# Last stage of a graph network kernel: residual adds on GpSimd, ScalarE on two groups, reciprocals by group

## What is computed

```python
exp_e = jnp.exp(e)                                     # e: score of each edge and head
denom = jax.ops.segment_sum(exp_e, trg, num_segments=n)
alpha = exp_e / (denom[trg] + 1e-10)
msg = h_prime[src] * alpha[:, :, None]
out = jax.ops.segment_sum(msg, trg, num_segments=n)    # (n, 8 * 32)
...
x = x + out                                            # x: (6250, 256) f32, the result
```

## Time and profile before

| | |
|---|---|
| median of 3 runs | 3204.86 us (3203.37 to 3205.41) |
| the profiled execution, span from first to last instruction | 3208.5 us |
| busy, share of the span: PE, DVE, ACT, POOL | 78%, 69%, 46%, 62% |
| from the start of the reciprocal (L1855) to the end of the span | 3174.19 to 3208.5 us |
| mean HBM traffic over the span | 116 GB/s |

### The profile page before, as it was taken

One profiled execution on the slowest core, in us unless ns is written; L12 is line 12 of the kernel. 1 busy time (PEld: TensorE's weight loads), 2 busy tenths in 40 slices (PEclk: granted clock), 3 DMA queues, 4 the chain that ended last, 5 costly groups with the idle time before them and its releaser, 6 DMA issues. The chain is left out here.

```text
span 3208.5 us, 81208 instructions
## 1 busy us (share of the span) xinstructions
PE 2491.2 (78%) x25602; PEld 2177.9 (68%) x25603; DVE 2207.3 (69%) x4515; ACT 1489.5 (46%) x3803; POOL 1998.7 (62%) x2143
## 2 busy tenths in 40 slices
PE   0577777777777699999999999966777777777773
PEld 0466666666666589999999999954555555555552
DVE  7777778877777646666666666647666667776766
ACT  5444444444444368888888888841111111111113
POOL 4677777777777534444444444427777777777772
PEclk9998889999989999999999999977889878889886
DMA  6555555555555400000000000006555655555554
GB/s 155 171 157 157 153 159 167 168 155 158 162 157 157 128 5 20 20 20 20 20 19 19 19 19 19 20 25 184 172 173 172 172 172 172 172 172 172 172 170 132
DMA packets 183839, 373.70 MB, mean 116 GB/s; under 512 B 42597, under 2 KB 93687, under 8 KB 183768
## 3 DMA queue, kind: packets, MB, share of 16 engines
q0 software_dynamic: 75552, 209.66, 23.1%
q1 hardware_dynamic: 107392, 162.37, 17.0%
q10 hardware_dynamic: 824, 0.87, 0.1%
HBM read 346.95 MB, written 25.80 MB: 116 GB/s over the span
## 5 line engine op out<-in xcount | busy, mean ns | idle before, releaser
L449 POOL DMA_INDIRECT rows<-tab_scratch,srcs x784 | 766.8, 978 | 238.7 <-issue 232.0
L1449 POOL DMA_INDIRECT a_rows<-tab_scratch,srcs x784 | 750.6, 957 | 251.9 <-issue 235.2
L1515 PE MATMUL sum_ps<-feat,a_hot 128*125 128x264 f32 x1960 | 608.8, 467 | 234.2 <-DVE feat L1607 116.5
L1515 PEld LDWEIGHTS sum_ps<-feat,a_hot 128*125 128x125 f32 x1960 | 423.3, 226 | 340.7 <-DVE feat L1607 128.6
L875 PE MATMUL z_ps<-ah,w 128*128 128x125 f16 x6400 | 553.6, 219 | 0.0
L875 PE MATMUL z_ps<-al,w 128*128 128x125 f16 x3200 | 542.4, 217 | 0.0
L875 PEld LDWEIGHTS z_ps<-ah,w 128*128 128x128 f16 x6400 | 489.6, 97 | 0.0
L1459 ACT ACTIVATE feat<-d 128x32 f32<-128x32 f32 x196 | 44.9, 229 | 826.5 <-DVE d L1603 578.9
L503 PE MATMUL mlp_ps<-ewa,eab 128*128 128x256 f16 x788 | 199.9, 287 | 266.4 <-PEq L499 265.1
L510 PE MATMUL sum_ps<-rows,hot 128*125 128x256 f16 x980 | 294.0, 300 | 81.5 <-DMA rows<-tab_scratch,srcs 56.1
L1059 ACT ACTIVATE a<-z,pack 128x125 f32<-128x125 f32 x800 | 321.5, 480 | 72.5 <-ACTq L1055 72.5
(11 more groups left out here) (206 smaller groups left out, 5533.7 us busy)
## 6 DMA issues: line engine op xcount, KB each, us to landing
ea<-edge_t SPq DMA_DIRECT2D x394, 128.0 KB
dstb<-dst_flat SPq DMA_DIRECT2D x98, 512.0 KB, 4.0
rows<-tab_scratch,srcs POOLq DMA_INDIRECT x784
a_rows<-tab_scratch,srcs POOLq DMA_INDIRECT x784
tab_scratch<-prow SPq DMA_DIRECT2D x50, 128.9 KB
hx<-x SPq DMA_DIRECT2D x50, 125.0 KB
x_scratch<-x SPq DMA_DIRECT2D x50, 125.0 KB
hs<-tab_scratch SPq DMA_DIRECT2D x50, 125.0 KB
```

What stands on the lines that cost most here:

```text
L449: pool.indirect_dma_start(rows[:, b % DEEP, k, :], None, dram["tab0"], bass.IndirectOffsetOnAxis(ap=srcs[:, c:c + 1], axis=0),).then_inc(r ...
L1449: pool.indirect_dma_start(rows[:, b % DEEP, k, :], None, dram["tab1"], bass.IndirectOffsetOnAxis(ap=srcs[:, c:c + 1], axis=0),).then_inc(r ...
L1515: ins = pe.matmul(out[:], hot[:, h, k, :], feat[:, row, k, :], start=(k == 0), stop=(k == CB - 1))
```

## The change

Five things change, all in `finish`:

- ScalarE multiplies groups 4 and 8 in place of 3, 6 and 9 and waits for each group's weights.
- GpSimd gets a program: it does the residual add and the tail for the groups 1, 4, 6 and 8 (`ON_POOL`), in this order. For 4 and 8 it waits for ScalarE (`normed`), for 1 and 6 for VectorE's multiply (`weighted`). It raises `pool_out`.
- VectorE takes the reciprocals by groups of 40 columns: first 4 and 0, then each group's own just before its multiply, and 8's after group 1's multiply. It multiplies eight groups and adds six. It no longer waits for ScalarE.
- SP stores in the order 0, 2, 1, 3, 4, 5, 7, 6, 9, 8, waiting for `pool_out` or `out_ready`.
- The slice of a group gets a helper, `chunk`.

```diff
--- before.py
+++ after.py
@@ -1787,11 +1787,19 @@
         top_ps = m.ps("top_ps", [P, 1])
 
         out_ready = m.sem("out_ready")
-        ON_ACT = (3, 6, 9)
+        ON_ACT = (4, 8)
+        ON_POOL = (1, 4, 6, 8)
+        FIRST_G = (4, 0)
+        STORES = (0, 2, 1, 3, 4, 5, 7, 6, 9, 8)
+        fits = 2 * D - TW
+
+        def chunk(i):
+            return slice(i * FB, (i + 1) * FB)
         out_stored = m.sem("out_stored")
         mx_ready, turned, mrow_ready, top_done = m.sem("mx_ready"), m.sem("turned"), m.sem("mrow_ready"), m.sem("top_done")
         exp_in, exp_ready = m.sem("exp_in"), m.sem("exp_ready")
         g_ready, normed = m.sem("g_ready"), m.sem("f_normed")
+        weighted, pool_out = m.sem("f_weighted"), m.sem("pool_out")
         chain_sem = m.sem("f_chain")
         HALF = 112
 
@@ -1800,9 +1808,12 @@
         @block.sync
         def _(sp):
             out_v = out.rearrange("(t p) c -> p t c", p=TN)
-            for i in range(steps):
-                tiles = slice(i * FB, (i + 1) * FB)
-                sp.wait_ge(out_ready, i + 1)
+            for i in STORES:
+                tiles = chunk(i)
+                if i in ON_POOL:
+                    sp.wait_ge(pool_out, ON_POOL.index(i) + 1)
+                else:
+                    sp.wait_ge(out_ready, len([j for j in range(i + 1) if j not in ON_POOL]))
                 for rows in (slice(0, HALF), slice(HALF, TN)):
                     sp.dma_start(out_v[rows, tiles, :], acc[rows, tiles, 0:D]).then_inc(out_stored, 16)
             sp.wait_ge(out_stored, 32 * steps)
@@ -1812,13 +1823,24 @@
             act.wait_ge(exp_in, 1)
             act.sem_inc(exp_in, -1)
             act.activation(g[:], c[:], ACT.Exp).then_inc(exp_ready, 1)
-            act.wait_ge(g_ready, 1)
-            for i in ON_ACT:
+            for n, i in enumerate(ON_ACT):
+                act.wait_ge(g_ready, n + 1)
                 for k in range(i * FB, (i + 1) * FB):
                     for h in range(HEADS):
                         a = acc[0:TN, k, h * HD:(h + 1) * HD]
                         ins = act.activation(a, a, ACT.Copy, scale=g[:, k, h:h + 1])
                 ins.then_inc(normed, 1)
+
+        @block.gpsimd
+        def _(pool):
+            for n, i in enumerate(ON_POOL):
+                a = acc[0:TN, chunk(i), 0:D]
+                if i in ON_ACT:
+                    pool.wait_ge(normed, ON_ACT.index(i) + 1)
+                else:
+                    pool.wait_ge(weighted, len([j for j in ON_POOL[:n + 1] if j not in ON_ACT]))
+                pool.tensor_tensor(a[:, :, 0:fits], a[:, :, 0:fits], acc[0:TN, chunk(i), TW:2 * D], ALU.add)
+                pool.tensor_tensor(a[:, :, fits:D], a[:, :, fits:D], x1_tail[:, chunk(i), :], ALU.add).then_inc(pool_out, 1)
 
         @block.tensor
         def _(pe):
@@ -1852,19 +1874,31 @@
             dve.wait_ge(exp_ready, 1)
             dve.sem_inc(exp_ready, -1)
             settled(dve.scalar_tensor_tensor(out=g[:], in0=g[:], scalar=GUARD, in1=acc[0:TN, :, D:TW], op0=ALU.mult, op1=ALU.add))
-            settled(dve.reciprocal(g[:], g[:]))
-            dve.sem_inc(g_ready, 1)
-            fits = 2 * D - TW
+
+            def weights(i):
+                settled(dve.reciprocal(g[:, chunk(i), :], g[:, chunk(i), :]))
+
+            for i in FIRST_G:
+                weights(i)
+                if i in ON_ACT:
+                    dve.sem_inc(g_ready, 1)
             for i in range(steps):
-                tiles = slice(i * FB, (i + 1) * FB)
-                a = acc[0:TN, tiles, 0:D]
+                a = acc[0:TN, chunk(i), 0:D]
                 a4 = a.rearrange("p t (h f) -> p t h f", h=HEADS)
-                if i in ON_ACT:
-                    dve.wait_ge(normed, ON_ACT.index(i) + 1)
-                else:
-                    settled(dve.tensor_tensor(a4, a4, g[:, tiles, :].unsqueeze(3).broadcast_to([TN, FB, HEADS, HD]), ALU.mult))
-                dve.tensor_tensor(a[:, :, 0:fits], a[:, :, 0:fits], acc[0:TN, tiles, TW:2 * D], ALU.add)
-                dve.tensor_tensor(a[:, :, fits:D], a[:, :, fits:D], x1_tail[:, tiles, :], ALU.add).then_inc(out_ready, 1)
+                if i not in ON_ACT:
+                    if i not in FIRST_G:
+                        weights(i)
+                    ins = dve.tensor_tensor(a4, a4, g[:, chunk(i), :].unsqueeze(3).broadcast_to([TN, FB, HEADS, HD]), ALU.mult)
+                    if i in ON_POOL:
+                        ins.then_inc(weighted, 1)
+                    else:
+                        settled(ins)
+                if i not in ON_POOL:
+                    dve.tensor_tensor(a[:, :, 0:fits], a[:, :, 0:fits], acc[0:TN, chunk(i), TW:2 * D], ALU.add)
+                    dve.tensor_tensor(a[:, :, fits:D], a[:, :, fits:D], x1_tail[:, chunk(i), :], ALU.add).then_inc(out_ready, 1)
+                if i == 1:
+                    weights(ON_ACT[1])
+                    dve.sem_inc(g_ready, 1)
 
 
 _PLAIN = ["x", "L0_gnn_eps", "L0_gnn_ee_w1", "L0_gnn_ee_b1", "L0_gnn_ee_w2", "L0_gnn_ee_b2", "L1_gnn_W"]
```

## The result

The changed kernel takes 3230.29 us (3228.89 to 3231.68, five runs), the kernel before beside it 3205.41 us (3203.37 to 3207.66). The ratio is 1.007, with a 95% interval of 1.0059 to 1.0081: slower by 19 to 26 us. The profiled execution has a span of 3227.1 us; its own time was 3228.89 us, 1.8 us above the span.

The account below looks back on a forecast made before the run. Only the last stage, bound by VectorE, was taken to change: 27.1 us of own work plus 9.3 blocked, then paired stores, end the span at 3217.7, +9.2 us; on the median 3204.86 that gives 3214.0, range 3209.5 to 3217.5.

Parts of the forecast that it names:

- VectorE's own work: Last stage: reciprocals by group, multiplies and six adds take VectorE 27.1 us against 29.97, without blocking.
- GpSimd's adds: Last stage: four adds of 1240 columns at 2.79 us each, and four 40-column tails at 0.25 us.
- The lock: Last stage: two-input VectorE instructions and GpSimd's adds exclude each other, blocking VectorE for 9.3 us, tails included.
- The replay: Last stage stepped through by the lock rule: VectorE blocked 1.7, 2.6, 2.2 and 2.6 us, ending at 3210.5.
- Rival (a): Last stage: the lock does not matter because strided adds interleave; -0.6 us, 3204.3; chance 0.06.
- (b): Last stage: the lock holds but costs less, some +5 us, 3210, within 0.2%; chance 0.20.
- (c): Last stage: GpSimd starves, its group 8 coming after VectorE's last tail; 3211.7 to 3212.9; chance 0.14.
- The stores: End of last stage: groups 7, 6 and 9, 8 leave in pairs, 2.2 us a group; span ends at 3217.7.
- The stage in sum: Last stage: blocking and paired stores together lengthen the span of 3208.5 us by 9.2 us.
- the first one: Opening step: the change touches only the last stage, so its possible gain is bounded by 30 us, 0.9% of the span.
- The upper end of 3217.5: Top of the forecast range for the time: nothing hides, +12.2 us, 3217.1, rounded up for the stores' rate.

Follow-up runs that it names:

- e3: Changed kernel with all ten adds back on VectorE, stores in order, VectorE waiting for ScalarE at groups 4 and 8: 3211.40 us, 1.0008 to the kernel before.
- e4: Changed kernel with each of GpSimd's four adds and tails replaced by one memset of 3300 columns, four groups' residual left out: 3218.69 us, one execution.
- e1: Changed kernel again, unaltered, on the same chip as e0: 3231.17 us, 1.0076 to the kernel before.
- e16: Changed kernel with one unused gather of 128 rows behind GpSimd's last add: 3220.69 us, 1.0035 to the kernel before.
- e12: Kernel before with one GpSimd add of 8 columns in the last stage, several executions: 3223.41 us, 1.0043 to the kernel before.
- e0: Kernel before again, unchanged, for a trace beside the others on one chip: 3206.73 us, 0.9998.
- e11: Kernel before with one GpSimd add of 8 columns ahead of the first gather of the second gather stage: 3212.28 us, one execution.
- e7: Kernel before with one GpSimd add of 8 columns in the last stage: 3219.15 us, one execution.
- e9: Kernel before with one GpSimd add of 8 columns right after the last gather, still in the second gather stage: 3222.57 us, one execution.
- e10: Kernel before with one GpSimd copy of 8 columns in the last stage: 3203.34 us, one execution.
- e13: Kernel before with one GpSimd copy of 8 columns in the last stage, several executions: 3210.98 us, 1.0000 to the kernel before.
- e8: Kernel before with one GpSimd add of 8 columns in the last stage and one memset of 8 columns behind it: 3224.58 us, one execution.
- e15: Kernel before with one GpSimd add of 8 columns, then one gather of 128 rows, waited for: 3214.36 us, one execution.
- e6: Kernel before with eight GpSimd memsets of 8 columns in the last stage: 3217.81 us, one execution.

## Why the prediction was right and wrong

- **VectorE's own work**: right. Reciprocals of 40 columns took 0.396 in the median for a forecast 0.41; e3's whole stage was 37.9 us for a sum of 37.8, and VectorE's part of e4's was 27.2 for 27.1.
- **GpSimd's adds**: 2.79 for 2.79. The tails wait and take 1.5 us in the trace, but cost VectorE only 0.07 on two of its own tails; the sum had 0.2 for all.
- **The lock**: right in kind, place and size. The replay had blocks of 1.7, 2.6, 2.2 and 2.6; the maxima and the timeline show 1.64, 2.59, 2.27 and 2.59. VectorE's last tail was forecast 36.3 us after the first reciprocal and came after 36.5. Rival (a) fell by the first stretched instruction, (b) by its size, (c) because GpSimd, each time that it waited, was let in when the VectorE instruction of the moment ended.
- **The stores**: right, last tail to end 7.6 for a forecast 7.2.
- **The stage in sum**: +9.2 forecast, +9.7 measured (+9.6 in e1); with e16's ending the whole kernel comes out 10.5 us above the kernel before beside it (7 to 15), where the forecast had 9.1.
- **The step that failed** is the first one: "the change touches only that stage, so what it can give is bounded by those 30 us". The sum put everything ahead of the stage at nothing, without a reason or a bound. The runs showed instead that the changed kernel's 1568 gathers ahead of the stage take 7 and 11 ns longer each, about 14 us, more than the stage's own 9.7; one add at the end of GpSimd's program, without the rest of the change, costs 0.43% (e12), 10 to 18 us. Why is open: the runs show when it happens, and that it comes by way of the next execution is inferred. No row of the kernel before could show the 957, since there GpSimd always ended with a gather. But its page did show that in two stages of 1000 us each GpSimd does almost nothing but such gathers, so that whatever touches a gather counts 1568 times. The upper end of 3217.5 came 13 us short.

## What to carry to other kernels

Before work moves to GpSimd, look for stretched instructions of VectorE beside its adds elsewhere in the trace. Where both engines read two tensors in SBUF, their times added up: 1.45 to 1.49 us taken from VectorE cost it 2.8 less the 0.2 to 1.2 us of reciprocals and settling that lay beside the add. Do not take every single-input instruction for free either. The reciprocals and the statistics ran through, but the kernel before has one that did not, in `nodes`, beside GpSimd's adds of 500 columns (start us, us; then ns min/median/max):

```profile
1796.03 1.56 POOL L828 TENSOR_TENSOR a<-a 128x500 f32<-128x500 f32 x1 [2.45 <-POOLq L827]
...
1796.71 1.03 DVE L1200 TENSOR_SCALAR hx<-hx,mv,rrow 125x256 f32<-125x256 f32 x1 [0.15 <-DVEq L1199]
...
L1200 DVE TENSOR_SCALAR hx<-hx,mv,rrow x50: 411/1029/1034, 1177.4 to 2148.7; 125x256 f32<-125x256 f32 x50
```

It has one tensor and two numbers per partition as inputs; its minimum is 0.41 us and its median 1.03.

Where one kind of instruction fills a stage hundreds of times back to back, compare its minimum and median in both traces first, in every stage, also where no line was changed. And look at what an execution ends with, not only at where it starts: here one add of 0.2 us at the end, which nothing waits for, went with 13 us more, and one gather and a wait after GpSimd's adds took some 12 us off again (e16).

## What the runs showed of the hardware that was not expected

- GpSimd's gathers of 128 rows take 942/946 ns (minimum, median) in both stages where no add of GpSimd follows the last gather of the execution (e0, e11). Where one does (e7, e9, e12), they take 949/953 (rows of 512 16-bit numbers) and 952/957 (rows of 264 32-bit numbers). One copy there doesn't do it (e10, e13), a memset behind the add doesn't undo it (e8), a gather with a wait behind it mostly does (e15, e16). What state or order is behind this stays open, and so does the 949 after several memsets (e4, e6).
- GpSimd's memset of 3300 columns, 2.85 us, doesn't disturb VectorE's two-input instructions (e4); its add of 1240 columns, 2.79 us, stops them.
- In the changed kernel neither engine starved. GpSimd's four 40-column tails each waited behind a VectorE instruction and ran when it ended, also the two before which VectorE left no gap between its add and its own tail (that tail took 0.26 for 0.19); VectorE's waiting instruction ran as soon as GpSimd's add ended, ahead of GpSimd's own tail.
